# Moving VectorE's layer-norm moments into a PSUM bank of their own, with all token reads in one bank

## What is computed

```python
concat = concatenate((x, 4 shifted copies of x), axis=1)        # 64 images, 10 channels of 104 x 104
normed = (concat - mean) * rsqrt(var + 1e-7) * gamma + beta     # one mean and variance for an image
h = conv(normed, W, 8x8 patches) + b                            # 169 tokens of 128 features for an image
h = concatenate([cls_tok, h], axis=1)
x = layernorm(h)                                                # over the 128 features, per token
q, k, v = x @ Wq.T, x @ Wk.T, x @ Wv.T
for token t:                                                    # images b, one shared memory S
    S   = S + 0.01 * sum_b v[b,t] k[b,t]^T
    out[b,t] = S q[b,t]
h = h + out
h = h + layernorm(h)          # the last block adds 2 * one_hot only where a mask holds
```

## Time and profile before

| | us |
|---|---|
| three executions, median (lowest to highest) | 237.27 (236.06 to 237.99) |
| the profiled execution, device time | 238.58 |
| its span, first to last instruction | 235.8 |
| outside the span | 2.78 |
| busy: PE, DVE, POOL, ACT | 204.5, 186.5, 160.9, 111.6 |

### The profile page before, as it was taken

The page is one execution under the profiler, slowest core; times in us unless marked ns, Lnnn a source line. Parts: engine busy times, 40 slices in busy tenths (PEclk is TensorE's granted clock), DMA queues, the critical chain, the costliest instruction groups (busy, mean ns, idle before and its releaser), DMA issues.

```text
span 235.8 us, 4919 instructions
## 1 busy us (share of the span) xinstructions
PE 204.5 (87%) x1558; PEld 171.5 (73%) x1558; DVE 186.5 (79%) x764; ACT 111.6 (47%) x243; POOL 160.9 (68%) x124
## 2 busy tenths in 40 slices
PE   0299996999899999999999999799989999967910
PEld 0289894877798899887877888698857888856700
DVE  1559981554497999999999999799989899797782
ACT  6012101444433466357537655556634755754460
POOL 1049979799963999948998489488996255432231
PEclk9999999999999999999999999999999999997795
DMA  6999939904040023151061601101101110121045
GB/s 173 374 429 424 417 159 167 372 0 153 0 151 6 0 92 111 29 170 44 3 195 44 200 14 33 44 20 29 44 3 44 46 44 11 40 46 44 0 103 126
DMA packets 16542, 25.98 MB, mean 110 GB/s; under 512 B 1319, under 2 KB 13277, under 8 KB 16262
## 3 DMA queue, kind: packets, MB, share of 16 engines
q1 hardware_dynamic: 16108, 25.31, 33.5%
q10 hardware_dynamic: 410, 0.38, 0.5%
HBM read 19.77 MB, written 5.92 MB: 109 GB/s over the span
## 4 chain that ended last, share of the span: by engine, by line
DVE 34%; PE 22%; POOL 15%; issue 12%; DMA 12%; ACT 2%; DVEq 1%; POOLq 0%; SPq 0%; ACTq 0%
DMA rows<-x_windows 12%; POOL scaled L381 10%; PE conv L457 8%; DVE state L735 5%; DVE state L727 5%; PE vr_ps L497 5%; DVE images L756 5%; DVE ln_shift L791 4%; DVE ln_stats L761 4%; PE first_ps L510 4%; POOL rstd L955 3%; PE out L527 3%; DVE scaled L381 2%; DVE var L747 2%; DVE ln_mv L776 2%
## 5 line engine op out<-in xcount | busy, mean ns | idle before, releaser
L457 PE MATMUL conv<-scaled,wt 128*128 128x256 f32 (+3 forms) x460 | 115.9, 372 | 10.1 <-DMA wt<-weight 10.1
L381 POOL TENSOR_TENSOR scaled<-rows,gam 128x832 f32<-128x832 f32 x60 | 93.7, 1584 | 5.6 <-PE conv L457 3.8
L457 PEld LDWEIGHTS conv<-scaled,wt 128*128 128x128 f32 x460 | 77.1, 193 | 18.2 <-DMA wt<-weight 10.1
L630 ACT ACTIVATE values<-vr_ps,rstd 128x256 f32<-128x256 f32 x85 | 40.1, 472 | 75.1 <-PE vr_ps L497 42.6
L955 POOL TENSOR_TENSOR rstd<-var,powers 128x9 f32<-128x9 f32 (+1 forms) x22 | 36.3, 1651 | 37.6 <-DVE var L747 37.1
L638 ACT ACTIVATE images<-images,ln_shift,ln_gain 128x128 f32<-128x128 f32 x81 | 38.3, 485 | 7.7 <-DVE ln_shift L791 6.1
L497 PE MATMUL vr_ps<-w_high,g_low 128*128 128x256 f32 x85 | 33.8, 398 | 7.7 <-ACT values L630 7.7
L727 DVE TENSOR_TENSOR state<-first_ps,state 128x128 f32<-128x128 f32 x83 | 24.0, 289 | 16.6 <-PE first_ps L510 11.1
L945 POOL TENSOR_TENSOR g_low<-g_t,g_high 128x512 fp32r<-128x512 f32 (+1 forms) x22 | 27.2, 1235 | 3.8 <-ACT g_high L617 3.8
L497 PEld LDWEIGHTS vr_ps<-w_high,g_low 128*128 128x128 f32 x85 | 16.2, 190 | 17.7 <-issue 16.3
L527 PE MATMUL out<-state,g_t 128*64 128x128 f32 x338 | 25.6, 294 | 2.1 <-DVE state L727 1.7
(11 more groups left out here) (112 smaller groups left out, 249.1 us busy)
## 6 DMA issues: line engine op xcount, KB each, us to landing
rows<-x_windows SPq DMA_DIRECT2D x13, 864.0 KB, 5.3
out<-images SPq DMA_DIRECT2D x42, 128.0 KB, 2.4
images<-x_rows SPq DMA_DIRECT2D x3, 624.0 KB, 20.7
images<-x_rows SPq DMA_DIRECT2D x1, 1456.0 KB, 13.2
images<-x_rows SPq DMA_DIRECT2D x1, 1248.0 KB, 15.6
images<-x_rows SPq DMA_DIRECT2D x1, 832.0 KB, 19.8
small<-smalls SPq DMA_DIRECT2D x1, 512.0 KB, 8.7
terms<-parked SPq DMA_DIRECT2D x3, 168.0 KB
```

The source lines that it names most:

```text
L381: return eng.tensor_tensor(scaled[:, s, at:at + N], window, gains, ALU.mult)
L457: last = pe.matmul(conv_ps[g % 2][:, at:at + n * B], wt[:, s], scaled[:, s, a % RING:a % RING + n], start=first, stop=(g < EARLY and s == ...
L630: act.activation(values[:, t % VALUE_SLOTS].rearrange("p a e -> p (a e)"), vr_ps[:, 0:2 * E], ACT.Identity, scale=rho_of(t)).then_inc(vr_r ...
```

## The change

The two banks for reads become one (`out_ps`), and the eighth bank, `dve_ps`, belongs to VectorE. The image statistics of the start move into it, and so do the means and variances of both layer norms (`ln1_mv`, `ln2_mv`) and a row of five ones (`unit`). The gain is formed from that row by another operation. Batches 20 and 22 of the 23 read batches go into `turn`, which is free by then. A batch of reads now waits until the results of the batch just before it have been added (the two before it, in the last two batches). The class token's column of the second layer norm moves from before group 0 to behind it, so that the power over both norms has eight columns and only in one case nine. The class token's read moves behind a stretch of convolution and behind the wait for `own_scales`.

```diff
-        ln1_mv = sb("ln1_mv", [P, TILES + 1, 2])
-        ln2_mv = sb("ln2_mv", [P, TILES + 1, 2])
...
-        out_ps = [pb("out0"), pb("out1")]
+        out_ps = pb("outs")
+        dve_ps = pb("dve")
...
-        stats = out_ps[1][:, 0:6 * len(STATS)].rearrange("p (a b) -> p a b", b=3)
-        weighted = out_ps[1][:, 6 * len(STATS):8 * len(STATS)]
+        stats = dve_ps[:, 0:6 * len(STATS)].rearrange("p (a b) -> p a b", b=3)
+        weighted = dve_ps[:, 6 * len(STATS):8 * len(STATS)]
+        ln2_mv = dve_ps[:, 0:2 * (TILES + 1)].rearrange("p (a b) -> p a b", b=2)
+        ln1_mv = dve_ps[:, 256:256 + 2 * (TILES + 1)].rearrange("p (a b) -> p a b", b=2)
+        unit = dve_ps[:, 500:500 + PER_GROUP + 1]
...
+        def out_bank(b):
+            return turn_ps if len(BATCHES) - b in (1, 3) else out_ps
...
         def ln2_part(buf, g):
-            return buf[:, g + BACK, PER_GROUP if g == 0 else PER_GROUP + 1:PER_GROUP + 1 + len(tiles_of(g))]
+            return buf[:, g + BACK, PER_GROUP:PER_GROUP + len(tiles_of(g)) + (g == 0)]
...
-                if t == BATCHES[b][0] and b > 0:
-                    pe.wait_ge(h2_ready, tile_no(BATCHES[b - 2][-1] if b > 1 else -1))
+                if t == BATCHES[b][0] and b == len(BATCHES) - 3:
+                    pe.wait_ge(h_ready, GROUPS)
+                elif t == BATCHES[b][0]:
+                    before = b - 2 if b > len(BATCHES) - 3 else b - 1
+                    pe.wait_ge(h2_ready, tile_no(BATCHES[before][-1] if b > 0 else -1))
...
-            pe.wait_ge(state_ready, 1)
-            pe.matmul(out_ps[1][:, 0:E], cls_t[:], state[:, STATE_SLOTS - 1, 1], start=True,
-                      stop=True).then_inc(out_done, 1)
             conv_shifts(EARLY - 1, 0, EARLY_SHIFTS)
             pe.wait_ge(own_scales_ready, 1)
+            pe.wait_ge(state_ready, 1)
+            pe.matmul(out_ps[:, 0:E], cls_t[:], state[:, STATE_SLOTS - 1, 1], start=True,
+                      stop=True).then_inc(out_done, 1)
             pe.wait_ge(terms_in, 16 * 2 * PRODUCTS)
...
-                dve.tensor_scalar(ln2_gain[:, a:z], ln2_part(rstd, g), 1.0, None, ALU.add)
+                dve.scalar_tensor_tensor(ln2_gain[:, a:z], unit[:, 0:z - a], 1.0, ln2_part(rstd, g), ALU.mult, ALU.add)
...
+            dve.memset(unit, 1.0)
...
-                    cols = 2 * PER_GROUP + 1
+                    cols = 2 * PER_GROUP + (back == 0)
```

More of the change, by code:

```diff
@@ L341, in states_to, with gain_of, shift_of @@
             return 1 + 2 * (t + 1)
+        def gain_of(t):
+            return ln2_gain[:, ln2_col(t):ln2_col(t) + 1]
+        def shift_of(t):
+            return ln2_shift[:, ln2_col(t):ln2_col(t) + 1]
+        def out_bank(b):
+            return turn_ps if len(BATCHES) - b in (1, 3) else out_ps
         def rho_of(t):
@@ L522, in read @@
                 b, at = batch_of(t), (t % PER_GROUP) * E
-                if t == BATCHES[b][0] and b > 0:
-                    pe.wait_ge(h2_ready, tile_no(BATCHES[b - 2][-1] if b > 1 else -1))
+                if t == BATCHES[b][0] and b == len(BATCHES) - 3:
[3 more added lines that the diff above has]
+                    pe.wait_ge(h2_ready, tile_no(BATCHES[before][-1] if b > 0 else -1))
                 for half in range(2 if t < TILES - 1 else 1):
                     a = half * B
-                    last = pe.matmul(out_ps[b % 2][a:a + B, at:at + E],
+                    last = pe.matmul(out_bank(b)[a:a + B, at:at + E],
                                      g_t[:, t // PER_GROUP % G_SLOTS, at + a:at + a + B], state[:, t % STATE_SLOTS, half],
@@ L554, in _ @@
             pe.wait_ge(centered, 3)
-            pe.matmul(out_ps[0][:, 0:E], wk_c[:], wq_c[:], start=True, stop=True, skip_group_check=True)
-            pe.matmul(out_ps[0][:, E:2 * E], center[:], small[:, WV], start=True, stop=True,
+            pe.matmul(out_ps[:, 0:E], wk_c[:], wq_c[:], start=True, stop=True, skip_group_check=True)
+            pe.matmul(out_ps[:, E:2 * E], center[:], small[:, WV], start=True, stop=True,
                       skip_group_check=True).then_inc(products_done, 1)
@@ L582, in _ @@
             pe.wait_ge(sums_ready, 2)
-            pe.matmul(out_ps[0][:, 2 * E:2 * E + 2], small[:, SAME], sums[:], start=True,
+            pe.matmul(out_ps[:, 2 * E:2 * E + 2], small[:, SAME], sums[:], start=True,
                       stop=True).then_inc(image_sums_done, 1)
@@ L586, in _ @@
             pe.wait_ge(scale_cols_ready, 1)
-            pe.matmul(out_ps[0][:, 0:B], scale_cols[:], small[:, IDENT, 0:B], start=True,
+            pe.matmul(out_ps[:, 0:B], scale_cols[:], small[:, IDENT, 0:B], start=True,
                       stop=True).then_inc(scale_rows_done, 1)
-            pe.wait_ge(state_ready, 1)
-            pe.matmul(out_ps[1][:, 0:E], cls_t[:], state[:, STATE_SLOTS - 1, 1], start=True,
-                      stop=True).then_inc(out_done, 1)
             conv_shifts(EARLY - 1, 0, EARLY_SHIFTS)
             pe.wait_ge(own_scales_ready, 1)
+            pe.wait_ge(state_ready, 1)
+            pe.matmul(out_ps[:, 0:E], cls_t[:], state[:, STATE_SLOTS - 1, 1], start=True,
+                      stop=True).then_inc(out_done, 1)
             pe.wait_ge(terms_in, 16 * 2 * PRODUCTS)
@@ L644, in finish_cls @@
                 act.wait_ge(ln2_affine_ready, 1)
-                act.activation(cls_result[:], cls_h2[:], ACT.Identity, scale=ln2_gain[:, 0:1], bias=ln2_shift[:, 0:1])
+                act.activation(cls_result[:], cls_h2[:], ACT.Identity, scale=ln2_gain[:, PER_GROUP:PER_GROUP + 1],
+                               bias=ln2_shift[:, PER_GROUP:PER_GROUP + 1])
             def step(t):
@@ L751, in add_out @@
                 g, at, a = t // PER_GROUP, (t % PER_GROUP) * E, P if t < TILES - 1 else B
-                bank = out_ps[batch_of(t) % 2]
+                bank = out_bank(batch_of(t))
                 dve.wait_ge(out_done, tile_no(BATCHES[batch_of(t)][-1]))
@@ L898, in _ @@
             dve.tensor_reduce(sums[:, 1:2], stat_tmp[:, 0], AX.X, ALU.add).then_inc(sums_ready, 1)
-            both = out_ps[0][:, 2 * E:2 * E + 2]
+            both = out_ps[:, 2 * E:2 * E + 2]
             dve.wait_ge(image_sums_done, 1)
@@ L909, in _ @@
                                      ALU.subtract).then_inc(image_var_ready, 1)
-            scale_rows = out_ps[0][:, 0:B]
+            scale_rows = out_ps[:, 0:B]
             a, z = 4 * TOKENS, TERM_ROWS
@@ L928, in _ @@
             for t in tiles_of(SECOND_LAST):
-                last = dve.tensor_scalar(tile_of(result, OUT_SLOTS, t), tile_of(h2, H2_SLOTS, t), ln2_gain[:, t + 1:t + 2],
-                                         ln2_shift[:, t + 1:t + 2], ALU.mult, ALU.add)
+                last = dve.tensor_scalar(tile_of(result, OUT_SLOTS, t), tile_of(h2, H2_SLOTS, t), gain_of(t),
+                                         shift_of(t), ALU.mult, ALU.add)
             last.then_inc(second_last_ready, 1)
```

16 lines of the change are left out of this document (9 added, 7 removed).

## The result

The changed kernel takes 230.91 us in the median (230.59 to 234.55), the kernel before 237.1 in the same comparison (236.06 to 237.99). The ratio is 0.974, 95% interval 0.968 to 0.979. The gain is 6.2 us; the forecast was 232.7 us, a gain of 4.6, in a range of 230.6 to 236.0. The profiled execution took 230.59 us with a span of 228.8 (before: 238.58 and 235.8). So 7.0 of the 7.99 us between these two lie in the span and 0.99 outside it, before the first or behind the last instruction (2.78 and 1.79 us).

What follows compares the result with a forecast made beforehand. PE sets the time; VectorE's lateness costs only through PE's stalls. Ceiling 5.4 us less 0.8 for GpSimd gives 4.6: profiled 238.58 becomes 234.0, median 237.27 becomes 232.7 us, whole range 230.6 to 236.0.

Steps and rivals of the forecast that it cites:

- What bounds it: Steady part: VectorE is late nearly everywhere but costs time only where that reaches PE, idle for 3.88 us.
- The ceiling: Most that PE's six stalls could give back: 3.9 us booked plus 1.5 under modelled ends, 5.4 us.
- The four operations: VectorE's L782, L791, L790 fall to 155 ns and L747 to 290, no longer waiting for GpSimd; 30.6 us less busy.
- PSUM's price: Extra cost of VectorE's small operations reading or writing PSUM: 0, upper bound 2.2 us of VectorE a period.
- What is late next: GpSimd, with 24.5 us of work against PE's 23.8 in three periods, nearly keeps pace; 0.8 us of stalls left.
- As a rival: GpSimd is the next limit: three stalls behind a power stay, only 1.4 us won, 235.9 us; chance 0.12.
- The power's columns: GpSimd's seventeen powers shorten by 2.7 us in all, mostly in its idle time; bounds 0 and 0.5 us.
- One bank for reads: PE holds reads until VectorE's additions end: cost 0 with 1.7 us of room, from 0.7 us up if VectorE stays late.
- The start and the end: Moved class token read and image statistics at the start, vr and values at the end: 0, bounds 0.3 us either side.
- The range: Forecast's own 230.8 (all 5.4 with bounds of power and ends) to 234.6; whole range 230.6 to 236.0 us.

Runs made afterwards that it cites:

- e1: The changed kernel with both layer norms' moments back in SBUF and the gain formed as before; 235.97 us, ratio 0.994 to the kernel before.
- e4: The changed kernel with only the gain formed as before, from SBUF to SBUF without the row of ones; 234.15 us, ratio 0.977.
- e8: The changed kernel with one more unread four-column power a group on GpSimd, ahead of the group's own power; 241.47 us, ratio 1.016.
- e6: As e1, with the power on nine columns again in every group; 236.46 us, ratio 0.9986 to the kernel before.
- e5: The changed kernel with the power on nine columns again in every group; 232.32 us, ratio 0.975 to the kernel before.
- e10: The kernel before with two unread matmuls on PE behind each vr of steps 72 to 80; 237.43 us, ratio 1.001.
- e11: The changed kernel with two unread matmuls behind each vr only in steps 73 to 78 that issue no products; 230.69 us, ratio 0.969.

## Why the prediction was right, point by point

**What bounds it.** Right. The chain named VectorE, but only PE's 3.88 us of idle time and what the modelled ends hide could be won. The ceiling was put at 5.4 us; the steady part became 5.46 shorter. The whole gain of 6.2 lies above that ceiling, by the time outside the span (below).

**The four operations.** Right: 155 ns was predicted and 154 to 162 measured, 290 and 281 for the one with scalar pointers, a busy time of about 156 and 156.4. e1 shows that it is the memory of the operands, and e4 that one tensor in SBUF with the output there is enough for a TENSOR_SCALAR to wait; the ends of the 34 long ones show for what. The prediction named the multiplications alone, and the subtraction L945 does the same. The Trainium skill (SBUF — State Buffer, Who interferes with whom) names both forms, two SBUF inputs and a `tensor_scalar` that uses both ports. The traces agree: L802 took at most 165 ns, where L782 took up to 1193.

**PSUM's price.** Taken as 0; the three operations without pointers take 1 to 9 ns more than L866's 153, and the means that are written to PSUM 165 ns where they took 157. The higher fixed cost of a PSUM source in the Trainium skill (VectorE: DVE Perf Modes, The TRN2 errata), an estimate of 65 ns more, is not seen here.

**What is late next.** The term of 0.8 us was mis-sized: no stall was left, 0 instead. GpSimd nearly out of room was right as a mechanism (e8). It starts its rows earlier once the powers come earlier: in the period of the products at 103.3 us the next multiplication starts at 104.50, where it started at 106.53 before beside products at 103.52. That this was what kept PE from stalling is argued. As a rival it had 0.12, and its price of 1.4 us for the gain did not come.

**The power's columns.** Mis-sized. I bounded them with 0.5 us. They are worth 1.77 us as long as VectorE is late (e1 against e6) and 0.06 us of the steady part once it is not (e5). As the last edit of a list they look useless and as the first good; the two gains do not add.

**One bank for reads.** Right: 0. The shortest room between the end of the additions (175.04 us) and the next reads (177.07) is 2.0 us as long as there is convolution to do, and at least 1.7 had been said. Behind it the periods are shorter and the room falls to 1.33 us (reads at 207.23) and 0.15 us (at 212.09), which the prediction did not look at. Even with VectorE late it costs nothing in the steady part (e6), less than the 0.7 us that I took from the earlier trace rows.

**The start and the end.** Right: 0 for both, once the clock is taken out. The profiled executions differ by 1.44 us in the end part, which is no work of the change. e6, which has the slow VectorE, ended its 52.87 us (181.73 to 234.6) like the changed kernel; it is the clock, which fell early in the one profile and not in the other. At a granted clock of 0.975 or more, 29 executions of the kernel before that ran beside the experiments have spans of 234.1 to 235.0 us, median 234.3, and the changed kernel's three have 228.8, 228.8 and 229.3. That is 5.5 us, the steady part's 5.46 and nothing else.

**Where the other 0.7 us come from.** They lie outside the span, a term that the prediction carried over unchanged at 2.78 us. It is 2.5 to 3.1 us in 25 of those 29 executions and 1.8 in the other four, but 1.8 or 1.9 in all four of the changed kernel. It is not VectorE's work: e10, the kernel before with unread matmuls added, has 1.8 us in all twelve executions. What sets it is open. So the gain of 6.2 exceeds the forecast of 4.6 by 0.9 us in the steady part, where no stall was left, and by 0.7 us outside the span, which is luck.

**The range.** The terms named for its lower end give 237.27 - 5.4 - 0.5 - 0.3 = 231.1 us, not the 230.8 written there, and the 230.6 of the whole range follows from no term. The measured 230.91 lies below that sum, by the time outside the span; without it the result would have been about 231.6.

## What to carry to other kernels

When small operations on VectorE take many times what their size explains, look at whether each long one ends just behind the end of an instruction of GpSimd (here 34 of 34). If so, give them a first operand in a PSUM bank, here one that only VectorE uses, and convert all that follow one another, for the wait moves to the next one that is left. And price such a change by the idle time of the engine with the most work: VectorE lost 30 us of busy time here, the kernel 6.

## What the runs showed of the hardware that I had not expected

A wait moves, which the prediction did not have (the expectation of e4 did): with only the gain left in SBUF, it took 868 ns in the mean instead of 283. TensorE's granted clock fell to 1.2 GHz in a part where PE idles for 0.66 us out of every 1.24, in some executions and not in others. With it the span of the kernel before went from 234.3 us up to 238.6. With ten unread matmuls in those gaps (e11) all six executions of the changed kernel stayed at 0.976 or more and within 0.25 us, at no cost. The time outside the span differed by up to 1.3 us between executions of one kernel (1.8 to 3.1 us), as much as some effects that one would measure with it: compare spans, too, and not device times alone.
